# Regrouping eight PSUM banks in a causal attention loop: two for scores and four for the row-maximum pass, in place of four and two

## The reference

```python
q, k, v = split(x @ w_qkv); q, k = rope(q), rope(k)
att = softmax(where(causal, (q @ k.T) * 16 ** -0.5, lowest))    # per head, 1024 x 1024
x = layernorm(x + (att @ v) @ w_proj)
x = layernorm(x + cross_attention(x, ctx))                       # 77 context rows
x = layernorm(x + w3(gelu(h2(gelu(h1(silu(w1 x) * (w2 x)))))))   # hidden width 1024
```

## Time and profile before

| what | us |
|---|---|
| median of 3 runs | 974.63 (972.71 to 979.38) |
| profiled execution, its time | 979.19 |
| its span from first to last instruction | 977.8 |
| self-attention steps 0 to 47, b = 0 | 75.7 to 237.6 |
| self-attention steps 0 to 47, b = 1 | 570.6 to 719.3 |
| mean granted TensorE clock | 0.895 |

### The profile page before, as it was taken

The page is one execution under the profiler, slowest core; times in us unless marked ns, Lnnn a source line. Parts: engine busy times, 40 slices in busy tenths (PEclk is TensorE's granted clock), DMA queues, the critical chain, the costliest instruction groups (busy, mean ns, idle before and its releaser), DMA issues. The chain is left out here.

```text
span 977.8 us, 13145 instructions
## 1 busy us (share of the span) xinstructions
PE 882.5 (90%) x4466; PEld 563.2 (58%) x4466; DVE 538.2 (55%) x1404; ACT 364.8 (37%) x770; POOL 363.0 (37%) x576
## 2 busy tenths in 40 slices
PE   5879999888889999999968789999998889999997
PEld 2545444334644788888745444543357257888886
DVE  3596788767676711441145967886167774116113
ACT  0314666454354421231103236665734443113110
POOL 4312224345345533353333122231362645335333
PEclk9965999769986999999979668997999699999999
DMA  9909201000000000000020000010000000000000
GB/s 305 336 7 401 72 2 46 2 1 1 2 5 0 1 1 1 1 1 1 22 94 1 1 2 2 2 45 2 1 1 4 3 1 1 1 0 22 1 1 24
DMA packets 15973, 34.61 MB, mean 35 GB/s; under 512 B 3483, under 2 KB 12392, under 8 KB 15720
## 3 DMA queue, kind: packets, MB, share of 16 engines
q1 hardware_dynamic: 15896, 33.63, 9.9%
HBM read 31.00 MB, written 13.63 MB: 46 GB/s over the span
## 5 line engine op out<-in xcount | busy, mean ns | idle before, releaser
L749 PE MATMUL bank<-hid_lo,ffn_w 128*128 128x512 f32 x512 | 202.2, 395 | 0.0
L878 ACT ACTIVATE prob<-bank 128x512 f32<-128x512 f32 (+3 forms) x384 | 164.2, 496 | 101.6 <-PE bank L550 100.9
L749 PE MATMUL bank<-hid_hi,ffn_w 128*128 128x512 f32 x512 | 201.6, 394 | 0.0
L1326 POOL TENSOR_TENSOR hid_lo<-act_raw,hid_hi 128x512 fp32r<-128x512 f32 x96 | 123.9, 1290 | 182.4 <-DVE hid_hi L1164 182.4
L1164 DVE CAST hid_hi<-act_raw 128x512 fp32r<-128x512 f32 x96 | 41.7, 435 | 212.4 <-ACT act_raw L964 211.3
L521 PE MATMUL bank<-k_t,q_t 64*128 64x512 f32 (+3 forms) x384 | 145.0, 496 | 13.0 <-DVE max_raw L1030 8.5
L1280 POOL TENSOR_SCALAR_AFFINE_SELECT prob<-prob 128x128 f32<-128x128 f32 x256 | 84.0, 344 | 180.5 <-ACT prob L878 177.9
L1030 DVE CUSTOM_DVE_ANT_0 bank<-bank,causal_bf 128x128 f32<-128x128 f32 (+3 forms) x256 | 122.3, 512 | 28.9 <-PE bank L521 26.8
L550 PE MATMUL bank<-q_t,k_t 64*128 64x512 f32 (+3 forms) x384 | 123.8, 438 | 0.9 <-issue 0.5
L964 ACT ACTIVATE act_raw<-bank,scales 128x512 f32<-128x512 f32 x64 | 44.2, 690 | 193.1 <-PE bank L749 193.1
L550 PEld LDWEIGHTS bank<-q_t,k_t 64*128 64x128 f32 x384 | 63.3, 211 | 82.5 <-ACT prob L878 47.5
(11 more groups left out here) (127 smaller groups left out, 1234.5 us busy)
## 6 DMA issues: line engine op xcount, KB each, us to landing
ffn_w<-scratch_h SPq DMA_DIRECT2D x2, 4096.0 KB, 23.2
ffn_w<-scratch_w SPq DMA_DIRECT2D x3, 1024.0 KB, 7.0
x_t<-in_x_t SPq DMA_DIRECT2D x2, 1024.0 KB, 5.2
x_tok<-in_x SPq DMA_DIRECT2D x2, 1024.0 KB, 5.5
out<-tok SPq DMA_DIRECT2D x16, 128.0 KB, 1.8
q_t<-max_rows SPq DMA_DIRECT2D x64, 4.0 KB
qx_t<-max_rows SPq DMA_DIRECT2D x64, 4.0 KB
w_qkv<-in_w_qkv SPq DMA_DIRECT2D x1, 768.0 KB, 6.9
```

Of the source, the lines that this page charges most:

```text
L749: o = mm(out[:], w_view(2 + layer, dt)[:, k, P * m:P * (m + 1)], view(src[part][:, k]), start=k + part == 0, stop=(k, part) == (KH - 1, 1))
L878: act.activation(prob[4 * (s % 2) + j][:, 0:n], S_BANK[j][:, 0:n], ACT.Exp, scale=SCALE).then_inc(S["exp_done"], 1)
L1326: pt(dst[1][:, r % 8], act_raw[n % 3][:], dst[0][:, r % 8].bitcast(F32), ALU.subtract).then_inc(S["act_lo"], 1)
```

## The change

Banks 2 and 3 alone hold scores, head j in bank 2 + j % 2. Banks 4 and 5 join banks 0 and 1 for the units from number 48 on (`M_BANK`, n % 4), and such a unit waits for the unit four before it. A score waits for the exponential two before it in the order of heads and steps: score(s, 2) for exp(s, 0), score(s, 3) for exp(s, 1), score(s+1, 0) for exp(s, 2), score(s+1, 1) for exp(s, 3). ScalarE reads the new bank. No instruction is added or removed, nor does any change its place in a queue; banks and wait values change. Cross-attention keeps its four score banks.

```diff
+    M_BANK = bank[0:2] + bank[4:6]
...
-        return bank[n % SHARED] if n < 2 * NU else A_BANK[n % 2]
+        return bank[n % SHARED] if n < 2 * NU else M_BANK[n % 4]
...
-            ahead = SHARED if p < 2 else 2
+            ahead = SHARED if p < 2 else 4
...
-            if s:
-                pe.wait_ge(S["exp_done"], 4 * (s - 1) + j + 1)
+            if s or j >= 2:
+                pe.wait_ge(S["exp_done"], 4 * s + j - 1)
...
-            mm(S_BANK[j][:, 0:CHUNK - q0], qkt(p, 1)[r, P * kb:P * (kb + 1)],
+            mm(S_BANK[j % 2][:, 0:CHUNK - q0], qkt(p, 1)[r, P * kb:P * (kb + 1)],
...
-                act.activation(prob[4 * (s % 2) + j][:, 0:n], S_BANK[j][:, 0:n], ACT.Exp, scale=SCALE).then_inc(S["exp_done"], 1)
+                act.activation(prob[4 * (s % 2) + j][:, 0:n], S_BANK[j % 2][:, 0:n], ACT.Exp, scale=SCALE).then_inc(S["exp_done"], 1)
```

## The result

| kernel | median us | runs | ratio to before | 95% interval |
|---|---|---|---|---|
| before | 975.83 (972.71 to 979.38) | 4 | | |
| changed | 989.75 (984.05 to 993.92) | 4 | 1.0156 | 1.0108 to 1.0203 |
| changed, on another occasion | 992.51 (989.43 to 993.53) | 5 | 1.0186 | 1.0159 to 1.0213 |

The profiled execution of the changed kernel took 984.05 us (span 982.4), 4.9 more than that of before (979.19). It is the fastest of its four, and it is the one with the highest mean clock: 984.05 us at 0.900, 986.74 at 0.888, 992.76 at 0.883, 993.92 at 0.880. So a profile of it shows where the banks cost and give, and less than usual of what the clock adds. One execution of the three-bank kernel with spare matmuls, further down, took 1148.16 us at a mean clock of 0.634, and its ratio leaves it out.

The account below looks back on a forecast made before the run. TensorE's in-order queue was taken as the bound, with units waiting for VectorE. Unit gain -14.4 us and score-bank prices +11.3 and +8.0 summed to +4.9: 979.5 us on the median, forecast range 973 to 986 (chance 0.46).

Parts of the forecast that it names:

- The price of two score banks: Scores wait for exponentials, score 2 until 1.24 us after score 0, score 3 until 1.73; +11.3 us in b = 1's steps 33 to 47.
- 1.4 for a stretch at half clock: Steps 37 to 41 of b = 1: the earlier window's half-clock stretch, priced at 1.4 us and left in.
- The price for b = 0: Steps 33 to 47 of b = 0: +8 us, bounds 3.0 and 11.3, since later scores overlap values' waits for selects.
- The gain of four unit banks: Steps with units: units no longer wait for their own step's reduction; -7.2 us a sequence, -14.4 for two.
- the score chain: Full unit steps: 1.73 us for score 3, 0.38 for it and its unit, then values, giving 3.10 a step.
- The sum: Whole kernel: -14.4 + 11.3 + 8.0 = +4.9 us, giving 984.1 for the profiled execution and 979.5 for the median.
- the rival with the falling clock: Steps without units: score waits idle TensorE, six to eight more steps at half clock, +10 us, 989.5; chance 0.23.
- "+2.5" for steps 37 to 41: Steps 37 to 41 of b = 1: 14.9 us against 12.43, with the half-clock stretch left in.
- "steps 16 and 17: 6.18 against 6.93": Unit steps 16 and 17: 2.48 + 3.70 = 6.18 us against 6.93, where units waited behind VectorE's staging copies.
- The sign set for the clock: Attention loop: the prediction is wrong if the loop's mean clock moves by more than 0.05.
- the argument against that rival: Steps 42 to 47 of the kernel before: as many waits there left the clock at 1.00.

Follow-up runs that it names:

- three-bank kernel with spare matmuls: Three score and three unit banks up to step 32, four score banks after, four spare matmuls in each of steps 34 to 40: 945.67 us, ratio 0.9692 to before.
- the kernel with the spare matmuls: Changed kernel plus four spare 512-column matmuls behind score 1 in each of steps 33 to 41: 983.75 us, ratio 1.0091 to the kernel before.
- The kernel with half the change: Two score banks as in the change, but units keep banks 0 and 1: 999.31 us, ratio 1.0269 to the kernel before.
- the kernel with both kinds: Changed kernel plus spare matmuls in steps 4, 16, 28 and in steps 33 to 41: 974.93 us, ratio 0.9994 to the kernel before.
- the late rows: Rows transpose moved behind score 3, on two score and four unit banks up to step 32, four score banks after: 955.56 us, against its base's 964.58.
- three and three: Three score and three unit banks up to step 32, four score banks after: 943.06 us, ratio 0.9656 to the kernel before.

## Why the prediction was right or wrong

**Where it was right.** *The price of two score banks* stood at 1.24 for score 2 and 1.73 for score 3, and step 18 shows 1.25 and 1.73. In the kernel with the spare matmuls (clock at 1.00) steps 33 to 47 of the second sequence take 47.79 us, +11.1 against 36.68, where the sum had +11.3. That sum held 1.4 for a stretch at half clock, so its steps at full clock were 1.2 too short together, most of it in 42 to 44 (12.30 where 11.85 stood) and 45 to 47. *The price for b = 0* (+8) measured +8.9, but not by its own terms: values waited 2.0 us for the selects in place of 8.3, so 6.3 of the price were absorbed where the sum took 3.3, and steps 37 to 41, at 0.50 where they had been at 0.60, cost 3.3. *The gain of four unit banks* was said to be held back by the score chain: steps 18 to 20 were put at 3.10 and took 3.16, and steps 12 to 23 at 34.6 and took 35.35 at full clock. The kernel with half the change shows that the gain is the units' and not the scores'. At a like clock steps 0 to 32 gave an estimated 5.6 us a sequence, where the sum had 6.4 for them. The sum, +4.9 us on the profiled execution's own time, came out at +4.9 between the two profiled executions. That equality is luck: the late steps cost 5.6 and 0.9 more than summed, and all that lies ahead of them gave back 20.7 instead of 14.4. In this execution the stretch at half clock around step 29 was absent in the first sequence, and in steps 0 to 5 the clock was 0.75 and 0.77 in place of 0.58, where the sum expected no gain of clock. A small slip beside it: VectorE's busy time in steps 12 to 23 adds up to 31.2 us, not 31.1.

**Where it was wrong.** The median rose by 14 us, to 989.75, and by 19 on the second occasion. The forecast of 979.5 was too low by 10, and the time lies where the rival with the falling clock had put it (989.5). The mechanism of the banks held; the term that was mis-sized is the one in the sum for the clock: "+2.5" for steps 37 to 41, which left one stretch at half clock "in", at 1.4 us. In its place the runs show a mean clock of 0.59 over 18.76 us. Steps 37 to 41 alone cost 6.3 us in the second sequence in place of 2.5. The same assumption stood unspoken under the gain: "steps 16 and 17: 6.18 against 6.93", at a clock of 1.00. They took 8.51 at 0.60 in the second sequence, and 8.5 and 8.6 in the profile of the second occasion. The rival had the mechanism, but looked for it only in the steps without units. It did not see that a unit step made shorter is one in which TensorE idles for a larger part: in steps 12 to 15 it is busy 10.34 of 11.70 us, where it was 11.70 of 12.00. The sign set for the clock, a mean of the loop moving by more than 0.05, could not have told: it was 0.83 and 0.88 before, 0.88 and 0.85 in the first profile and 0.82 and 0.84 in the second. The falls show stage by stage.

**What the argument against that rival was worth.** It said that in steps 42 to 47 of the kernel before as many waits left the clock at 1.00. The rows don't bear that: TensorE is busy 8.26 of 8.26 us and 9.27 of 9.27 there, so it did not idle at all, and only weight loads waited. In the changed kernel it does idle there, 0.74 and 0.75 us in steps 42 and 43, and the clock is 0.99 and 1.00 in the second sequence of the first profile. But in the first sequence of the second profile it is 0.80 in steps 42 to 44. The projections fill part of these steps; that what lies around a wait decides, and not the wait alone, fits this, but no run isolates it. The Trainium skill's page "TensorE: Matmul & The Clock Gate", section "A second HAM failure mode: psum-queue depth-cycling", said that the clock swings where short idles come between groups of matmuls while PSUM banks are cycled. The traces agree: 15 to 20 us at half clock in steps 37 to 41 with such idles, none in the second sequence once they were filled.

**What stays open.** In the first sequence the clock still falls in steps 33 to 41 with the spare matmuls, and in the kernel with both kinds part of the fall moved to steps 42 to 44. In the first sequence values wait for the selects beside VectorE's check pieces (3.8 us, three times, with the spare matmuls), which was not taken apart. Why the late rows gain 9 us on two and four banks is not shown either, and neither is what the spare matmuls would gain in the kernel before.

## What to carry to other kernels

A bank taken from one ring of PSUM buffers costs where the ring's wait enters a queue that other work stands in, so lay out the banks by stage: the same exchange gave 1% where both rings were in use and cost 3% where one had gone out of use, and three and three in place of four and two gave 3.4%. When waits are added to or taken from TensorE's queue, put down the granted clock of each stage as a term of its own. To tell such a term from the rest, fill the waits with spare matmuls into a free bank: if the clock holds and the time falls, it was the clock. Put them into the kernel before as well, or the comparison credits the change with clock that the kernel before had to win too.

## What the runs showed of the hardware

- The granted clock fell to 0.50 in a stretch where TensorE never idled for more than 0.75 us at a time (steps 33 to 41 of the changed kernel's second sequence, by the matmuls' modelled ends; in the first sequence a wait of 1.97 us for a select stands ahead of it). Steps 37 to 41 took 18.76 us at a mean of 0.59, and 13.69 at 1.00 with four spare matmuls a step.
- Nine spare matmuls of 512 columns in a sequence, all of them in a wait, took 14.8 us off the kernel (992.51 to 977.71).
- A step that gets shorter can get slower: steps 12 to 23 took 35.3 us at full clock and 37.5 where it fell, against 36.9 in the kernel before, where it held in both sequences and TensorE was busy 35.4 us of them, against 32.3 of the 35.3.
- The same instructions on the same banks can run at different clocks in one execution: steps 24 to 32 took 28.65 us at 1.00 in the first sequence and 31.79 at 0.84 in the second, in the kernel with the change from step 33 on.
